# The cross-attention mask added by GpSimd in SBUF instead of by two matmuls, in a decoder layer with a hand-kept order of work

## What is computed

```python
x = layernorm(x + self_attention(x, qkvw, qkvb, ow, ob))
scores = einsum('bsgrd,btgd->bgrst', xq, xk) / sqrt(16)
scores = scores + mask                       # [128, 128], same for every head
probs = softmax(scores)
x = layernorm(x + einsum('bgrst,btgd->bsgrd', probs, xv))
routing = softmax(x @ gate_w.T)
y = (x * (routing @ in_scale)) @ sign(w).T * (routing @ out_scale) + bias
out = layernorm(x + y)
```

## Time and profile before

| | |
|---|---|
| median of 3 runs | 377.65 us (376.38 to 379.04) |
| the profiled execution: time / span in its profile | 376.03 us / 374.2 us |
| busy TensorE, matmuls | 336.7 us (90%), 2788 instructions |
| busy VectorE | 255.8 us (68%) |
| busy ScalarE | 158.6 us (42%) |
| busy GpSimd | 121.8 us (33%) |
| mean granted clock of TensorE | 0.993 |

### The profile page before, as it was taken

One profiled execution on the slowest core, in us unless ns is written; L12 is line 12 of the kernel. 1 busy time (PEld: TensorE's weight loads), 2 busy tenths in 40 slices (PEclk: granted clock), 3 DMA queues, 4 the chain that ended last, 5 costly groups with the idle time before them and its releaser, 6 DMA issues.

```text
span 374.2 us, 7676 instructions
## 1 busy us (share of the span) xinstructions
PE 336.7 (90%) x2788; PEld 240.9 (64%) x2788; DVE 255.8 (68%) x825; ACT 158.6 (42%) x309; POOL 121.8 (33%) x203
## 2 busy tenths in 40 slices
...
GB/s 269 381 138 242 205 62 5 54 138 253 173 189 87 4 12 37 185 248 207 178 97 2 36 15 167 252 214 192 33 16 23 4 105 123 114 4 4 2 0 56
DMA packets 25846, 42.32 MB, mean 113 GB/s; under 512 B 7421, under 2 KB 17801, under 8 KB 23505
## 3 DMA queue, kind: packets, MB, share of 16 engines
...
## 4 chain that ended last, share of the span: by engine, by line
PE 65%; DVE 16%; DMA 6%; issue 4%; POOL 4%; ACT 3%; SPq 1%; POOLq 0%; DVEq 0%; ACTq 0%
PE bank_a L905 7%; PE bank_a L907 7%; PE bank_a L906 7%; DVE nma L723 5%; PE bank_b L1051 4%; PE bank_b L1062 4%; PE bank_a L991 3%; PE bank_a L978 3%; PE bank_b L1054 3%; PE bank_b L1052 3%; PE bank_b L1039 3%; DVE x L795 3%; PE bank_b L1036 2%; POOL owL L561 2%; PE bank_b L999 2%
## 5 line engine op out<-in xcount | busy, mean ns | idle before, releaser
L614 ACT ACTIVATE pb<-bank_b 128x512 f32<-128x512 f32 x64 | 38.0, 599 | 56.2 <-PE bank_b L1054 40.8
L606 ACT ACTIVATE pa<-bank_a 128x512 f32<-128x512 f32 x64 | 36.0, 596 | 35.2 <-PE bank_a L978 28.4
L795 DVE CUSTOM_DVE_ANT_0 x<-bank_b,mraw 128x128 bf16<-128x128 f32 x192 | 41.9, 286 | 4.0 <-DMA out_dram<-x 2.2
L723 DVE TENSOR_REDUCE nma<-bank_a 128x4 f32<-128x512 f32 x64 | 39.9, 682 | 3.0 <-PE bank_a L961 2.8
L905 PE MATMUL bank_a<-xH,wH 128*128 128x256 f32 x128 | 37.0, 289 | 3.6 <-DVE xL L704 3.6
L906 PE MATMUL bank_a<-xL,wH 128*128 128x256 f32 x128 | 36.2, 283 | 0.0
L907 PE MATMUL bank_a<-xH,wL 128*128 128x256 f32 x128 | 36.2, 283 | 0.0
L1051 PE MATMUL bank_b<-idr,mH 128*128 128x512 f32 x64 | 34.6, 541 | 1.0 <-DMA qx<-mrb 0.5
L905 PEld LDWEIGHTS bank_a<-xH,wH 128*128 128x128 f32 x128 | 24.7, 193 | 4.2 <-DVE xL L704 4.2
L1052 PE MATMUL bank_b<-idr,mL 128*128 128x512 f32 x64 | 25.2, 394 | 0.0
L1054 PE MATMUL bank_b<-qx,kx 99*128 99x512 bf16 x64 | 25.0, 391 | 0.0
...
## 6 DMA issues: line engine op xcount, KB each, us to landing
...
```

The lines of the kernel that those rows point to most:

```text
L614: act.activation(pb[:, n % NPB, :], pb_bank(i, *step)[:], ACT.Exp).then_inc(*rb.is_empty(i, *step))
L723: dve.tensor_reduce(nma[:, b, 4 * j:4 * j + 4], pa_bank(i, *step)[:].rearrange("p (m t) -> p m t", m=KT), AX.X, ALU.max, negate=True).then ...
L795: last = dve.tensor_tensor_reduce(unread[:, part * P:(part + 1) * P], pb_bank(i, *step)[:, r * P:(r + 1) * P], mraw[:], -1.0, -LOWEST, ALU ...
```

## The change

In thread B's `st`, TensorE makes the scores alone, with one matmul a tile. ScalarE copies the bank to pb without an exponential. GpSimd then adds the transposed mask, mT, to pb in place. A new step `ex` has ScalarE take the exponential of pb in place, and `pv` waits on that. mT is made once by a transpose in step `mask`. In `s` of group 3 the mask's two matmuls stay. The table is rewritten throughout: the eight `ex` of a sequence stand behind their `st`, four by four, and `st` and `s` steps of both threads have other places. UNREAD is empty. At the start, the loads of the biases and the gate move from SyncE's queue to ScalarE's, 14, 8 and 30 transposes that nobody reads stand ahead of `small`, `xt` and the first `q`, VectorE makes both halves of the first x instead of sharing with ScalarE, the first `xt` stands ahead of the weights' split, and GpSimd takes half of the low parts of two of three weight blocks. Three pairs of small buffers of the two threads become one each.

```diff
 ORDER = steps("""
-    C0.small C0.w:0 A0.xt:0 A0.xt:1 A0.lc B0.cp:0 B0.cp:1 A1.lc C0.w:1 C0.w:2 A0.q:0 A0.q:1 A0.ldq:0 A0.q:2 A0.q:3 C0.ow
+    C0.small A0.xt:0 A0.xt:1 C0.w:0 C0.w:1 A0.lc B0.cp:0 B0.cp:1 C0.w:2 A0.q:0 A0.q:1 A0.ldq:0 C0.sign A0.q:2 C0.swt:1
...
-UNREAD = {("C", 0, "swt", 3): 10, ("C", 0, "vb"): 11, ("A", 0, "s", 0, 0): 8, ("A", 0, "mt", 0): 6, ("A", 0, "st", 0, 0): 5,
...
+UNREAD = {}
...
+                elif thread == "B" and name == "st":
+                    b, g = step[1:]
+                    n = (GB * i + b) * HT + g
...
+                    rb.wait_emptied(pool, i, *step)
+                    scores = pb[:, n % NPB, :].rearrange("p (r t) -> p r t", r=4)
+                    pool.tensor_tensor(scores, scores, mT[:].rearrange("p (o t) -> p o t", o=1).broadcast_to([P, 4, P]),
+                                       ALU.add).then_inc(masked, 1)
...
+                elif thread == "C" and name == "w" and step[1] != 1:
+                    blk = step[1]
+                    for kt in range(WSPLIT, KT):
...
+                        pool.tensor_tensor(low, raw, high, ALU.subtract).then_inc(w_low_p, 1)
...
-                        act.activation(pb[:, n % NPB, :], pb_bank(i, *step)[:], ACT.Exp).then_inc(*rb.is_empty(i, *step))
+                        act.activation(pb[:, n % NPB, :], pb_bank(i, *step)[:], ACT.Copy).then_inc(*rb.is_empty(i, *step))
+                elif thread == "B" and name == "ex":
+                    b, g = step[1:]
+                    n = (GB * i + b) * HT + g
+                    act.wait_ge(masked, n + 1)
+                    act.activation(pb[:, n % NPB, :], pb[:, n % NPB, :], ACT.Exp).then_inc(probs, 1)
...
+                    if i == 0 and name in ("xt", "q") and step[1] == 0:
+                        for _ in range(8 if name == "xt" else 30):
+                            pe.transpose(dst[:, 0:P], idf[:], idf[:])
...
-                    ident4 = idr[:].rearrange("p (o t) -> p o t", o=1).broadcast_to([P, 4, P])
-                    pe.matmul(d4, mH[:], ident4, start=True, stop=False)
-                    pe.matmul(d4, mL[:], ident4, start=False, stop=False)
                     a = 4 * (g % 2)
-                    pe.matmul(d4, kx[0:SM, b, g, :], qx[0:SM, b, a:a + 4, g // 2, :], start=False, stop=True).then_inc(*rb.is_full(i, *step))
+                    pe.matmul(d4, kx[0:SM, b, g, :], qx[0:SM, b, a:a + 4, g // 2, :], start=True, stop=True).then_inc(*rb.is_full(i, *step))
                 elif thread == "B" and name == "pv":
...
-                    rb.wait_emptied(pe, i, "st", b, 4 * u + 3)
+                    pe.wait_ge(probs, (GB * i + b) * HT + 4 * u + 4)
```

More of the change, by code:

```diff
@@ L39 @@
 MASKED = NG - 1
+WSPLIT = KT // 2
 def steps(table):
@@ L51 @@
 ORDER = steps("""
-    C0.small C0.w:0 A0.xt:0 A0.xt:1 A0.lc B0.cp:0 B0.cp:1 A1.lc C0.w:1 C0.w:2 A0.q:0 A0.q:1 A0.ldq:0 A0.q:2 A0.q:3 C0.ow
-    A0.v:0 A0.v:1 C0.scales C0.sign C0.swt:3 A0.ldk:0 C0.swt:0 A0.ldk:1 A0.ldq:1 C0.mask C0.vb A0.xb A0.s:0,0 A0.s:0,1
-    A0.s:0,2 A0.s:0,3 A0.s:0,4 A0.s:0,5 A0.s:0,6 A0.s:0,7 C0.swt:1 C0.swt:2 A0.mt:0 C0.rows A0.s:1,0 A0.s:1,1 A0.s:1,2
-    A0.s:1,3 A0.st:0,0 A0.s:1,4 A0.s:1,5 A0.st:0,1 A0.s:1,6 A0.pv:0,0 A0.s:1,7 A0.st:0,2 A0.st:0,3 A0.pv:0,1 A0.st:0,4
@@ L107 @@
-NO_BANK = ("xb", "lc", "cp", "ldq", "ldk", "ldx", "ldc", "n1", "n2", "n3", "w", "ow", "mask", "sign", "rows", "scales")
+    C0.small A0.xt:0 A0.xt:1 C0.w:0 C0.w:1 A0.lc B0.cp:0 B0.cp:1 C0.w:2 A0.q:0 A0.q:1 A0.ldq:0 C0.sign A0.q:2 C0.swt:1
+    A0.q:3 A0.ldk:0 A0.ldq:1 A0.ldk:1 C0.swt:3 C0.swt:2 C0.scales A0.v:0 C0.mask C0.ow A0.v:1 C0.vb A0.s:0,0 A0.s:0,1
+    A0.s:0,2 A0.s:0,3 A0.s:0,4 A0.s:0,5 A0.s:0,6 A0.s:0,7 A0.mt:0 A0.s:1,0 A0.s:1,1 A0.s:1,2 A0.s:1,3 C0.swt:0 A0.st:0,0
+    A0.st:0,1 A0.st:0,2 A0.s:1,4 A0.pv:0,0 A0.xb A0.st:0,3 A0.pv:0,1 A1.lc A0.st:0,4 A0.s:1,5 A0.pv:0,2 A0.st:0,5
@@ new lines @@
+    A0.s:1,6 A0.pv:0,3 C0.rows A0.s:1,7 A0.st:0,6 A0.st:0,7 A0.pv:0,4 A0.pv:0,5 A0.pv:0,6 A0.pv:0,7 A0.mt:1 A0.ot:0,0
+    A0.ot:0,1 A1.xt:0 A1.xt:1 A0.ct:0 B0.ctx:0 B0.ctx:1 A0.st:1,0 A0.st:1,1 A0.op:0 A0.n1:0 A0.st:1,2 A0.st:1,3 B0.ldc:0
+    A0.pv:1,0 A0.pv:1,1 A0.st:1,4 A0.pv:1,2 A0.pv:1,3 A0.st:1,5 A0.st:1,6 A0.st:1,7 A0.pv:1,4 B0.xt:0 B0.ldx:0 A0.pv:1,5
+    A0.pv:1,6 A0.pv:1,7 A0.ot:1,0 A0.ot:1,1 A1.q:0 A1.q:1 A1.ldq:0 A1.q:2 A0.ct:1 A1.q:3 A1.ldq:1 B0.s:0,0 A1.v:0
+    B0.s:0,1 B0.s:0,2 A1.ldk:0 B0.s:0,3 B0.s:0,4 B0.s:0,5 B0.s:0,6 B0.s:0,7 A0.op:1 A0.n1:1 B0.mt:0 A1.ldk:1 B0.xt:1
@@ L180, in decoder_layer @@
         mL = sb("mL", [P, P], F32R)
+        mT = sb("mT", [P, P], F32)
         idf = sb("idf", [P, P], F32)
@@ L572, in _ @@
                     u = step[1]
+                    if i == 0:
+                        continue
                     ra.wait_full(act, i, *step)
@@ L853, in _ @@
                     blk = step[1]
-                    for kt in range(KT):
+                    for kt in range(KT if blk == 1 else WSPLIT):
                         dve.wait_ge(w_high, KT * blk + kt + 1)
@@ L867, in _ @@
                 elif thread == "C" and name == "mask":
+                    rb.wait_full(dve, 0, "mask")
+                    dve.tensor_copy(mT[:], pb_bank(i, "mask")[:, 0:P]).then_inc(*rb.is_empty(i, "mask"))
                     dve.wait_ge(ld_mask, 16)
@@ L1032, in _ @@
                     if i >= MASKED:
+                        if i == MASKED and b == 0 and g == 0:
+                            pe.wait_ge(masks, 3)
                         d4 = dst[:].rearrange("p (r t) -> p r t", r=4)
@@ L1101, in _ @@
                     pe.wait_ge(idents, 1)
+                    dst = pb_bank(i, "small")
+                    for _ in range(14):
+                        pe.transpose(dst[:, 0:P], idf[:], idf[:])
                     pe.wait_ge(ld_small, 48)
                     pe.wait_ge(bias_permuted, 1)
-                    dst = pb_bank(i, "small")
                     pe.transpose(dst[:, 0:2 * KT], bperm[:], idf[0:2 * KT, 0:2 * KT])
```

153 lines of the change are left out of this document (84 added, 69 removed).

## The result

The changed kernel takes 423.6 us (median of 4 runs, 417.7 to 424.4) against 377.2 us (4 runs) for the kernel before: ratio 1.115, 95% interval 1.109 to 1.121. It is 46 us slower. The forecast said 367.5 us and faster, with a range of 351 to 384 us. The time moved the other way and lies far outside the range. The profiled execution took 424.35 us, with a span of 422.3 us and a mean granted clock of 0.855. It counts as a slow run; the ratio compares fast runs alone, whose clock was 0.875 to 0.879, and makes the loss 43 us.

A forecast was written before the change was run, and what follows sets the result against it. The prediction took TensorE to bound the middle, with VectorE nearly as full where maxima stand thick. From 376.0 us, -14.5 (middle), -1 (start) and +7 (end) gave 367.5 us; whole range 351 to 384 us.

The forecast's parts named there:

- TensorE bounds the middle: In the three middle stretches, 74.2 to 311.7 us, PE is busy 71.96 of 74.0, 73.83 of 75.5, 82.63 of 88.0 us.
- middle, mask off TensorE: -14.5 us: Three middle groups: 7 us gained beside the maxima plus 2.5 us in each group outside them, from 22.4 us of matmuls.
- VectorE's maxima bound: Rival, chance 0.15: only some 5 us go in the middle, 377.0 us, no change.
- The detour: Middle groups: copy, add and exponential per tile; four adds take 5.1 us on GpSimd, halving a 5 us gain per group.
- The end, +7 us: Thread B alone, first `s` of group 3 to last `pv`: 4.9 us of longer chain over 38.7, 2.1 us of clock.
- The halves: End: four halves of copy, four adds, exponential and `pv`, 7.4 us each, where before a half took 4.4 us.
- no longer than before: Test for the end: if it came out no longer than before, GpSimd's queue was not its chain.
- The clock, chance 0.06: Rival, chance 0.06: PE falls to half clock in the stretches of maxima, 7 us longer in each group, 388.5 us.
- likewise if a clock near 0.5 stands in a middle window: Test for the middle groups: a clock near 0.5 in one of their windows would show the forecast wrong.
- Start, -1 us: Start: 1.86 us of unread matmuls go, against PE pausing ahead of `vb` and through the first maxima; ends -4 and +3.
- The rule on GpSimd and VectorE: The 82 us of new adds slow some of VectorE's SBUF work; the sum had nothing for it apart from the halves taken.
- 369.9 us: Whole kernel instead of 367.5 us, at 0.48 us for each of some 5 GpSimd and VectorE meetings a group, none hidden.

The follow-up runs named there:

- b_no_mask: The kernel before without the two mask matmuls of `st` and nothing in their place: 370.6 us, ratio 0.979.
- a_warm: The kernel after with 144 unread matmuls put where PE waits: 406.2 us, ratio 1.076.
- b_new_table: The kernel before, its start's code included, with only the new table (without `ex`) and no unread matmuls: 429.7 us, ratio 1.135.
- b_no_unread: The kernel before with UNREAD emptied, the mask still on TensorE: 384.8 us, ratio 1.014.
- b_new_end: The kernel before with the new order, without `ex`, only from the first `s` of thread B's group 3 on: 395.9 us, ratio 1.048.
- a_no_add: The kernel after without GpSimd's 64 adds, copy and exponential kept, mask missing from the probabilities: 413.3 us, ratio 1.092.
- b_new_way: The changed kernel with the table and unread matmuls of before, `ex` behind every four `st`, seven `st` moved: 472.1 us, ratio 1.247.

## Why the prediction was wrong

Two steps failed most: the new table, which had no term in the sum and costs some 50 us, and the gain in the middle.

**"TensorE bounds the middle"** is the first step that failed. It rests on 97% of busy time, and b_no_mask shows what that share was worth: 22.4 us of matmuls taken away, 1.3 us gained. The mean clock of b_no_mask, 0.961 over 369.4 us, puts some 29 us at half the clock, 24 more than in the profiled run before. At 0.2 to 0.24 us each, the rate of a_warm, that ate at most some 5 to 6 us (an estimate). The gain from the matmuls in the term "middle, mask off TensorE: -14.5 us" should have been -1, or at most -7 with the clock kept, and not 22 less a cost. The term was too large by its own premises as well: if half of the tiles lie in the thick of the maxima, only half of each group's 7.5 us is left outside it, 3.7 and not 5, which makes 18 us and not 22. What sets the period instead, the chains of a group's steps or VectorE's maxima, no run here separates. In b_no_mask PE's waits grew at thread A's maxima (nma, 1.3 to 4.0 us), at their split (npa, 0.9 to 2.5 us) and at banks that thread B's exponentials empty (ahead of `st`, none to 2.3 us). The second rival, "VectorE's maxima bound", was nearer for the middle.

**The detour, "half of 5 us for each group, 2.5 us".** It was sized from durations, which were right, and from PE's cover, which was not. In the old order the path costs 94 us, of which the add 61, waited for at `pv` and at the split of the maxima. The forecast's 5 us, halved, stood for one round of four adds in a group, but a group has four such rounds; and the small steps queued behind the adds on GpSimd had no price in the middle. For the new order I should have asked what it gives up to avoid that.

**The new table had no term at all.** This is the largest error. I read the order of steps for where the new operations went and took the rest as free. With the old path and the old code it costs 45 to 51 us (b_new_table, against b_no_unread and against before): 18 in the end and behind it (b_new_end), the rest in groups 1 to 3 and the start. In the kernel after, some 15 to 17 us of such a loss is the clock. Which steps of the table cost it stays open, but for the second sequence's scores in the end and owL in the start.

**The end, +7 us.** It measured +16. The kernel after from 349 us on, all engines:

```profile
349.75 0.24 POOL L488 TENSOR_TENSOR npb<-nr_,npb 128x32 bf16<-128x32 f32 x1
...
350.14 0.23 PE L1009 MATMUL bank_b<-idb,npb 128*96 128x128 bf16 x1 [1.65 <-POOL npb L488]
...
354.29 2.06 ACT L639 ACTIVATE pb<-bank_b 128x512 f32<-128x512 f32 x4 [5.16 <-PE bank_b L1092]
...
354.63 1.78 SPq L351 DMA_DIRECT2D qx<-scr_x  x3
...
356.43 5.12 POOL L525 TENSOR_TENSOR pb<-pb,mT 128x512 f32<-128x512 f32 x4
356.50 1.48 DVE L727 TENSOR_SCALAR x<-x,mvb,rsb 128x512 f32<-128x512 f32 x1 [1.00 <-POOL rsb L495]
...
360.42 0.76 PE L1078 MATMUL bank_b<-mH,idr 128*128 128x512 f32 x1 [4.87 <-issue]
```

The reader can follow it: `ldx` of the second sequence waits for the sum behind `B2.ff:1`, and the last split at 349.75 and its transpose at 350.14 stand ahead of `B2.ff:1`, so the second sequence's `qx` is asked for only at 354.63, and its scores start at 360.42, 20.2 us after the first sequence's (12.8 in the kernel before). The copies start at 354.29, but the add only at 356.43, because GpSimd's queue has the layer norm's step before it. In the sum I had the second sequence's scores beside the first's halves at no cost. The halves I priced at 7.4 us each. The four `pv` of the end start at 364.26, 373.12, 384.34 and 393.11 us, 8.9, 11.2 and 8.8 us apart, where before it was 4.4. The add is not all of it: without it (a_no_add) the end is still 52.5 us, and with the old path in the new order it is 51.9 to 53.8 us in four kernels, with `pv` up to 11.3 us apart. Nor is the order all of it: with the new path in the old order (b_new_way) it is 55.1 us, with `pv` 8.9 to 9.8 us apart, and 44.4 us without the add. Either cause alone makes the end some 52 to 55 us long, and both together no longer. By my own test, that the end would be "no longer than before" if GpSimd's queue was not its chain, I would have read the longer end as proof of the queue, which the test does not give; a_no_add shows that in this order the queue was not needed for it. With the clock at 0.66 in the end of the kernel after and 0.73 in that of a_no_add, PE's own pieces run up to twice as long; in a_warm, at 0.91, the end is 52.2 us, so the clock is at least 2.6 us of it.

**The clock, chance 0.06.** "Against it: even there PE would be over half busy." The clock fell none the less, to 0.91, 0.90 and 0.93 in the three groups. My sentence "likewise if a clock near 0.5 stands in a middle window" looked for it in one place; it came in short stretches all over. It made some 15 to 17 of the 43 to 46 us. The rival's 21 us was about the right size for the whole kernel, by luck: it put them in the three groups, which have some 44 of the 122 us at half the clock, and nothing more in the start and the end, which have the rest. Its chance was much too small.

**Behind the last `pv`** the sum had no term, and 3.5 us came; emptying UNREAD in the kernel before (b_no_unread) makes 2.7 us there.

**Start, -1 us:** +7.9 us. PE stood 8.3 us ahead of `vb`, until GpSimd had made owL. That is the new order's (8.4 us in b_new_table, with the old start's code). The unread matmuls, whose removal I had counted as 1.9 us gained, are worth 4.0 us of the start in the old order (b_no_unread). Some 24 us of the start lie at half the clock (0.15 of 82.1 us, twice). a_warm, with 28 unread matmuls there, had 78.2 for 82.1 us.

**The rule on GpSimd and VectorE.** VectorE's normalisation of 512 columns took 0.82 us on average in the kernel after (L727, above) and 0.57 us without the add:

```profile
L718 DVE TENSOR_SCALAR x<-x,mvb,rsb 128x512 f32<-128x512 f32 x16 | 9.0, 568 | 4.0 <-POOL rsb L495 4.0
```

Five of the sixteen ran wholly beside adds, and took 1.45 to 1.49 us (four) and 0.77 us; with GpSimd idle one takes 0.52 to 0.55 us. Thirty of the maxima, read from PSUM, ran wholly beside adds and took 0.67 to 0.69 us, as without. The Trainium skill, GPSIMD Engine Reference, section 8 (Key points), has the two engines share SBUF interfaces and contend when VectorE runs in a 2-port mode or has two SBUF inputs. The trace agrees that they contend over SBUF; in which mode this instruction ran, no run shows. It is 4.0 us of VectorE's time, a small part of the loss. In the prediction, 369.9 us was a slip: 5 meetings of 0.48 us are 2.4 us in one group, some 7 in three. There were 5 meetings in all, each dearer.
